# A Mamba-style scan layer in chunks of 512 tokens: the front of a chunk is issued beside the scans of the chunk ahead of it, with its weights streamed from DRAM

## The reference, cut to what matters

```
xn   = layernorm(modulated x)
z    = xn @ W_in                         # 512 channels
gate = silu(xn @ W_gate)
dt   = clip(softplus(z @ W_dt + b_dt), 0.001, 1.0)
Bp, Cp = z @ W_B, z @ W_C                # 16 states each
for t:  h = exp(dt_t * A) * h + dt_t * B_t * z_t      # 512 channels x 16 states
        y_t = sum over states of h * C_t
x1 = x + g * ((y * gate) @ W_out)
```

## Time and profile before

| | us |
|---|---|
| median of 3 runs | 3269.24 (3268.8 to 3269.72) |
| the profiled execution's own time | 3268.99 |
| its span, first to last instruction | 3267.0 |

### The profile page before, as it was taken

How to read it: one execution, slowest core, us unless ns; L and a number is a source line. 1 busy time by engine, 2 the same in 40 slices (tenths; PEclk the granted TensorE clock), 3 DMA queues, 4 the chain that set the end, 5 groups by cost and what they waited for, 6 DMA issues and landing times.

```text
span 3267.0 us, 45469 instructions
## 1 busy us (share of the span) xinstructions
PE 2928.0 (90%) x14848; PEld 2392.1 (73%) x14848; DVE 2684.9 (82%) x4436; ACT 2109.7 (65%) x3852; POOL 1969.2 (60%) x1701
## 2 busy tenths in 40 slices
PE   7576799998999999899999999899999989999898
PEld 4355577787877778687777778777777878777776
DVE  3968989797988979798898979799897979989441
ACT  3555486776758676675767667675866767585443
POOL 1857667475766757565776756566675756666110
PEclk8577699999999999999999999999999999999998
DMA  4241132231422232232313233131332323133122
GB/s 130 82 163 58 50 109 69 98 114 65 141 78 97 76 111 97 87 122 69 110 62 117 91 112 107 65 112 67 111 101 98 107 73 123 59 104 118 46 89 90
DMA packets 152787, 308.56 MB, mean 94 GB/s; under 512 B 18372, under 2 KB 96988, under 8 KB 135144
## 3 DMA queue, kind: packets, MB, share of 16 engines
q1 hardware_dynamic: 152008, 302.52, 27.7%
q0 software_dynamic: 272, 1.57, 0.1%
q10 hardware_dynamic: 272, 1.57, 0.1%
HBM read 288.27 MB, written 17.35 MB: 94 GB/s over the span
## 4 chain that ended last, share of the span: by engine, by line
PE 31%; DVE 28%; issue 18%; ACT 14%; POOL 4%; DMA 2%; DVEq 1%; POOLq 0%; SPq 0%; ACTq 0%
DVE acc L1495 12%; DVE hs L1531 10%; PE ps_B L1771 8%; PE ps_A L1771 7%; PE ps_H L1766 4%; PE ps_H L1784 4%; PE ps_B L1766 3%; ACT ps_A L1302 2%; POOL bu L1151 2%; PE ps_B L1924 2%; PE ps_B L1784 2%; PE ps_B L1876 2%; DVE hA L1725 2%; DMA ws_in<-w_split 1%; ACT nn L727 1%
## 5 line engine op out<-in xcount | busy, mean ns | idle before, releaser
L1151 POOL TENSOR_TENSOR bu<-z,bb 128x512 f32<-128x512 f32 x1024 | 1294.5, 1285 | 344.5 <-DVE hs L1531 286.5
L1531 DVE TENSOR_TENSOR_SCAN hs<-ps_A,state,bu 128x512 f32<-128x512 f32 x768 | 976.1, 1276 | 26.4 <-ACT ps_A L1302 12.9
L1302 ACT ACTIVATE ps_A<-dt,a_neg 128x512 f32<-128x512 f32 x1024 | 700.1, 687 | 450.4 <-DVE hs L1531 448.5
L1766 PE MATMUL ps_H<-ident,hs 128*128 128x128 f32 x4096 | 653.4, 295 | 203.3 <-DVE acc L1495 113.5
L1766 PEld LDWEIGHTS ps_H<-ident,hs 128*128 128x128 f32 x4096 | 522.6, 152 | 348.6 <-DVE acc L1495 151.5
L1495 DVE SCALAR_TENSOR_TENSOR acc<-ps_H,ctok,acc 128x512 f32<-128x512 f32 x960 | 699.5, 730 | 32.7 <-PE ps_H L1766 31.9
L1876 PE MATMUL ps_B<-ws_out,hid 128*128 128x256 f32 x2944 | 694.8, 381 | 2.4 <-ACT hid L1354 2.2
L1876 PEld LDWEIGHTS ps_B<-ws_out,hid 128*128 128x128 f32 x2944 | 535.7, 191 | 66.6 <-ACT hid L1354 2.6
L1771 PE MATMUL ps_B<-fh,ws_in 128*128 128x512 f32 x1440 | 534.8, 417 | 9.2 <-DMA ws_in<-w_split 4.6
L1771 PEld LDWEIGHTS ps_B<-fh,ws_in 128*128 128x128 f32 x1440 | 270.7, 188 | 68.1 <-DVE bl L1686 7.9
L1531 DVE TENSOR_TENSOR_SCAN hs<-ps_A,bu 128x512 f32<-128x512 f32 x256 | 310.5, 1215 | 10.5 <-POOL bu L1151 6.0
(11 more groups left out here) (351 smaller groups left out, 4806.8 us busy)
## 6 DMA issues: line engine op xcount, KB each, us to landing
ws_in<-w_split SPq DMA_DIRECT2D x126, 1024.0 KB, 6.3
bb<-b_rows SPq DMA_DIRECT2D x256, 256.0 KB, 3.6
ws_out<-in_L_ffn_V_rwkv SPq DMA_DIRECT2D x64, 512.0 KB, 5.3
ws_out<-in_L_ffn_W SPq DMA_DIRECT2D x32, 512.0 KB, 8.1
xb<-in_L_attn_x SPq DMA_DIRECT2D x16, 512.0 KB, 6.3
n<-in_L_attn_x SPq DMA_DIRECT2D x16, 512.0 KB, 4.1
w_split<-wsp SPq DMA_DIRECT2D x8, 1024.0 KB, 5.6
out<-xb SPq DMA_DIRECT2D x16, 512.0 KB, 3.0
```

The costliest lines, as they stand in the source:

```text
L1151: pool.tensor_tensor(bu[:, u % 4, :], z[:, d, :], bb[:, s % 2, :], ALU.mult)\
L1302: act.activation(b.t[:, :], dt[:, d, :], ACT.Exp, scale=a_neg[:, d, s:s + 1])\
L1531: dve.tensor_tensor_scan(hs[:, s % 2, d, :], b.t[:, :], bu[:, k % 4, :], state[:, s, d:d + 1] if i % CPB else 0.0, ALU.mult, ALU.add)\
L1766: return pe.transpose(dst, src, ident[:, :])
```

## The change

**Steps.** The marks are gone. A chunk's own list now begins at unit 8. Units 0 to 7 of chunk i+1 are issued among the last steps of chunk i: units 0 to 3 in four new steps "end", each with the last read-out of a channel tile of chunk i, units 4 to 7 in the four y steps. The transposes of state 0 and ACT's copy of them into acc come as four steps "turn0" after out. A chunk has 71 steps instead of 98.

**Front.** Its pieces are due some 20 steps earlier, beside the last units of the chunk ahead (PE: dt and z at -19 to -17 of a step list in which unit 60 is at -19; gates at -10 to -2, after y). The gate products come last.

**Memory.** z, dt and ctok are doubled; bu gets its own buffer; yT is written over gate. The DRAM row buffer of B is doubled. The resident w_in and w_dt are gone: three more slots of 1 MB (dt, z, gt) are written to DRAM once, and read back for every chunk from 1 on, into ws_in[0], ws_in[1], ws_in[0], through SP's queue.

**Banks.** The front's products use B0 and B1, between the experts' up-products and f. 

**Small.** Table loads of ACT are written out for ln, silu, gelu and back to exp/tanh; the bids' Sigmoid becomes Exp(-x) on ACT and an add and a reciprocal on DVE. Chunk 0's norms move from the first block into the second. All PACE values are new.

```diff
-UNIT_STEPS = [("unit", u) for u in range(DS * DB + DB)]
-TAIL_STEPS = [("y", k) for k in range(DB)] + [("out", 0), ("out", 1), ("x1", 0)]
+UNIT_STEPS = [("unit", u) for u in range(2 * DB, DS * DB)]
+END_STEPS = [("end", d) for d in range(DB)]
+TAIL_STEPS = [("y", k) for k in range(DB)] + [("out", 0), ("out", 1), ("x1", 0)] + [("turn0", t) for t in range(NT)]
...
+AT0 = len(UNIT_STEPS) - N_S
...
 BANK_USES = {
-    "A0": FRONT[0::2] + [f"dA{u}" for u in range(0, DS * DB, 2)],
-    "A1": FRONT[1::2] + [f"dA{u}" for u in range(1, DS * DB, 2)],
+    "A0": [f"dA{u}" for u in range(0, DS * DB, 2)],
+    "A1": [f"dA{u}" for u in range(1, DS * DB, 2)],
+    "N0": FRONT[0::2],
+    "N1": FRONT[1::2],
...
-        w_in = {h: sb(f"w_in_{h}", [P, KC, 2 * DI], F32R) for h in "hl"}
-        w_dt = {h: sb(f"w_dt_{h}", [P, KC, DI], F32R) for h in "hl"}
...
-        bu = over("bu", [P, 4, CT], "xnh")
+        bu = sb("bu", [P, 4, CT])
...
-        z = sb("z", [P, DB, CT])
-        dt = sb("dt", [P, DB, CT])
+        z = sb("z", [P, 2 * DB, CT])
+        dt = sb("dt", [P, 2 * DB, CT])
...
-        yT = over("yT", [P, DB, CT], "hs", skip=4 * DB * CT)
+        yT = gate
...
@@ SP, n_stream
+                    for h, name in enumerate(("dt", "z")):
+                        yield name
...
+                            take(sp, i - 3, ("p3", "p7")[h])
+                        front_in(i, name)
+                    yield "bc"
+                    since(sp, s_bu, i - 1)
+                    used(sp, i, "bc")
+                    sp.dma_start(b_rows[i % 2], bcs[DS:2 * DS, :]).then_inc(s_bw.sem, 16)
...
+                    yield "gt"
+                    if i:
+                        take(sp, i, "dt2")
+                        take(sp, i, "dt3")
+                        front_in(i, "gt")
...
@@ ACT, n_stream
+                    for k in range(DB):
+                        yield f"gate{k}"
+                        if k == 0:
+                            load_table(act, "silu")
+                        if i:
+                            take(act, i - 1, "wo0")
+                            take(act, i - 1, "wo1")
...
@@ DVE, step
+                    if name == "end":
+                        if i + 1 < NCH:
+                            scan(i + 1, k)
+                        if i >= 0:
+                            read_out(i, DS - 1, k)
                     if name == "y":
...
+                        if i + 1 < NCH:
+                            scan(i + 1, DB + k)
```

More of the change, by code:

```diff
@@ L48 @@
 NSLOT = len(SLOTS)
+TABLES = {"exp tanh": 0, "exp ln": 6, "gelu": 10, "silu": 18}
+FRONT_SLOTS = ["dt", "z", "gt"]
 CREDIT = 1
@@ new lines, in scan @@
+                def scan(i, k):
+                    s, d = k // DB, k % DB
+                    if d == 0 and s >= 1:
+                        inputs_made(sp, i, s)
+                        if s < DS - 1:
+                            load_b(i, s + 1)
+                        elif i + 1 < NCH:
+                            load_b(i + 1, 0)
+                    if (s, d) == (DS // 4, 1) and i % CPB == 0:
+                        since_x1(sp, i)
+                        sp.dma_start(w_out[:, :, :], kp(w["L0_attn_W_out"])).then_inc(s_wout.sem, 16)
@@ new lines, in step, with front_in @@
+                    if name == "end" and k == 0 and 0 <= i < NCH - 1:
+                        inputs_made(sp, i, DS)
+                        load_b(i + 1, 1)
+                    if name == "y" and i + 1 < NCH:
+                        scan(i + 1, DB + k)
+                def front_in(i, name):
+                    dst = ws_in[1 if name == "z" else 0]
+                    sp.dma_start(dst[:, :, :, :].bitcast(F32).rearrange("p h k m -> p (h k m)"),
+                                 w_split[NSLOT + FRONT_SLOTS.index(name)]).then_inc(s_wf[name].sem, 16)
@@ L1108, in w_stream @@
                 def w_stream(_):
+                    yield "front"
+                    for n, src in enumerate((ws_in[0], ws_in[1], w_gt0)):
+                        sp.dma_start(w_split[NSLOT + n], src[:, :, :, :].bitcast(F32)
+                                     .rearrange("p h k m -> p (h k m)")).then_inc(v_front, 16)
                     yield "fold"
@@ new lines, in keep_state, with scan @@
+                def keep_state(i, s):
+                    for u in (s * DB + DB - 2, s * DB + DB - 1):
+                        used(act, i, f"dA{u}")
+                    act.activation(state[:, s, :], hs[:, s % 2, :, CT - 1], ACT.Copy).then_inc(s_state.sem, 1)
+                def scan(i, k):
+                    s, d = k // DB, k % DB
+                    if d == 2 and s >= 1:
+                        keep_state(i, s - 1)
+                    if s == 0:
+                        act.wait_ge(s_dt.sem, s_dt.at(i, d + 1))
+                    b = fill(act, i, f"dA{k}")
+                    act.activation(b.t[:, :], dt[:, i % 2 * DB + d, :], ACT.Exp, scale=a_neg[:, d, s:s + 1])\
+                       .then_inc(b.full, 1)
@@ L1304, in step @@
[L1304 to L1315 removed]
+                        scan(i, k)
@@ new lines, in step @@
+                    if name == "end":
+                        if k == 2 and i >= 0:
+                            keep_state(i, DS - 1)
+                        if i + 1 < NCH:
+                            scan(i + 1, k)
+                    if name == "y" and i + 1 < NCH:
+                        scan(i + 1, DB + k)
+                    if name == "turn0" and i + 1 < NCH:
+                        b = take(act, i + 1, f"hT{k}")
+                        if k == 0:
+                            used(act, i + 1, "ct")
+                            if i >= 0:
+                                take(act, i, "y2")
+                                take(act, i, "y3")
+                        act.activation(acc[:, k, :], b.t[:, :], ACT.Copy, scale=ctok[:, (i + 1) % 2, k, 0:1])\
+                           .then_inc(b.free, 1)
@@ new lines, in step @@
+                    if name == "end":
+                        if i + 1 < NCH:
+                            scan(i + 1, k)
+                        if i >= 0:
+                            read_out(i, DS - 1, k)
+                    if name == "y":
+                        if i + 1 < NCH:
+                            scan(i + 1, DB + k)
+                        if i >= 0:
+                            used(dve, i, f"gt{k}")
+                            b = take(dve, i, f"y{k}")
+                            dve.tensor_tensor(yT[:, k, :], b.t[:, :], gate[:, k, :], ALU.mult).then_inc(b.free, 1)
```

526 lines of the change are left out of this document (259 added, 267 removed), and 128 rows, old and new, of the table PACE.

## The result

The changed kernel takes 3366.39 us (median of 4 runs, 3358.77 to 3368.56) against 3269.02 for the kernel before on the same chip (3267.75 to 3269.72): a ratio of 1.0294, 95% interval 1.0276 to 1.0312. The forecast was 3124 us with a range of 3060 to 3215. It is slower by 97 us where 145 less were expected. The profiled execution has a span of 3366.0.

A forecast was written before the change was run, and what follows sets the result against it. PE was taken to bound the turn and DVE the scans; overlapping them gives 129.5 + 142 + 13 x 181 + 162 = 2786.5 against 2936.7, saving 150.2, less 5.7 in the head: 3124 us, range 3060 to 3215.

The forecast's parts named there:

- The bound changes hands: Middle chunk: PE ends last at the turn while DVE idles 19 us, DVE in the scans while PE idles 9.3.
- the lower bound is 175.3: Middle chunk: PE's load 175.3 us is the floor, 188.6 the upper bound; PE at 97% gives 181.
- DVE's scans fill its hole at the turn: Turn: eight scans of the next chunk, 10.2 us of DVE work, move into DVE's idle time there.
- PE's front fills its hole at the experts' end: Scans: 13 front products, 17.9 us plus 1.0 of transposes, move from the turn into PE's idle time.
- 129.5 from the first scan: Chunk 0, first scan to gate product: 119.3 us plus eight scans of chunk 1; chunk 1's front hidden by scans.
- Chunk 1, 142: Gate product 0 to 1: DVE bounds it, load stays, DVE fills some 96%; 174.4 us becomes 142.
- ACT at the turn: Rival: unit 8 waits for two ACT table changes, 5.4 us in each of 14 chunks, giving 3200; chance 0.10.
- The last interval, 162: Chunk 15's interval, without front or next scans: PE 156.4 us, at 97% 161, taken as 162.
- Tail unchanged at 241.4: After the last gate product: the same x and f work in the same order, so 241.4 us stays.
- Streaming at zero: Front weights, 3 MB more a chunk, load under cover at no cost; without cover 18.9 us a chunk.
- exposed loads at 3408: Rival: PE stands until weight loads land; all three exposed cost 284 us, giving 3408; chance 0.07.
- Displacement: Rival: front matmuls in the scans delay transposes DVE needs; chunk stays at 188, giving 3215; chance 0.13.

The follow-up runs named there:

- the useless products: Changed kernel plus five groups of eight useless PE products a chunk, ahead of the keys' group and the four transposes behind it; 3319.05 us, ratio 1.0159.
- the run without it: Changed kernel with the second modulation product issued ahead of chunk 0's four gate products, on banks B2 and B3; 3350.39 us, ratio 1.0252.

## Why the prediction was wrong

Point by point, by its own steps:

- **"The bound changes hands ... a chunk costs the sum of both bounds"**, and with it "the lower bound is 175.3 ... I take PE at 97%": this is the step that failed. Busy shares of 93 and 98% were read as two rates that could be evened out. But PE's share at the turn was high because the front stood there, as the one work that waited for almost nobody; take it away and what is left are transposes and short groups, each waiting for the last. PE is busy for 92% of a middle chunk instead of 97, idle for 15.6 us of the turn's 64. Half of the front's products could be dropped, and of the 8.3 us came 1.1 and 2.4. Size: 13 x 10.2 = 133 us of the 242 by which the forecast missed; the head has 26 of them, chunk 1 28, the last interval 19 and the tail 37.
- **"DVE's scans fill its hole at the turn"** came true and was worth nothing: DVE's busy time rose from 47.9 to 51.9 of the turn's 64 us, and a chunk with 3.7 us more of DVE takes no longer.
- **"PE's front fills its hole at the experts' end"** came true in part: the waits for acc fell from 73.8 to 45.6 us over thirteen chunks, and new ones at the turn outweighed them.
- **The granted clock** stood in its own rows (0.80 where DVE closed the experts) and entered no term. The changed kernel could have gained 3.5 us a chunk by it. It is not why the change was slower, for in the middle chunks both kernels have the same mean clock, 0.96 and 0.97. The Trainium skill ("TensorE: Matmul & The Clock Gate", Part 1, The HAM clock gate) says that the throttled state is the default and that activity releases it, and its table "Why this matters for your kernels" advises against gaps of idle time in mid-kernel. By that rule more work at a sparse turn should raise the clock, and the traces agree: 0.82 in the changed kernel, 1.00 with the useless products.
- **Chunk 0, "129.5 from the first scan"**: measured 159.4 (90.7 to 250.1). The first scan came earlier than the 94.6 forecast, at 90.7. The scans then stopped for the modulation product, priced as 5.3 us that "come back": it went in behind the gates on shared banks, stopped DVE for 10.4 and brought its work on the rows with it; its order was worth 16 us in all. Behind it stood the wait for ACT, 13.2 us in the run without it. And five scans, not eight, stand ahead of gate product 0.
- **Chunk 1, 142**: measured 170.0, with DVE busy 137.1 and PE 122.8. The hole at the turn stayed. Here the rival "ACT at the turn" shows bare, with no x stream to hide it, behind two waits for the products out:

```profile
262.81 0.69 DVE L1604 TENSOR_TENSOR xb<-ps_H,xb 128x512 f32<-128x512 f32 x1 [5.74 <-PE ps_H L1848]
266.27 0.69 DVE L1604 TENSOR_TENSOR xb<-ps_H,xb 128x512 f32<-128x512 f32 x1 [2.76 <-PE ps_H L1848]
276.56 1.28 DVE L1578 TENSOR_TENSOR_SCAN hs<-ps_A,state,bu 128x512 f32<-128x512 f32 x1 [7.67 <-ACT ps_A L1336]
```

  The scan of unit 8 waits 7.67 us for ACT, which waits for wo1, the gates and the tables first. In middle chunks DVE's norms of x lie over this, and this scan waits 0.97 us. Over thirteen middle intervals DVE's waits for decay factors came to 68.4 us, none longer than 1.8, as against 10.8 before; no run shows what they cost.
- **The last interval, 162**: 181.3. PE's work was sized nearly right, 161.4 us for 156.4, but it filled 89% instead of 97: the turn's 64 us hold 48.3 of PE, as in a middle chunk.
- **"Tail unchanged at 241.4 ... comes in the same order"**: 278.5, the order was not the same. The diff holds the new due times; they were not read against the old ones. With the old order it is 242.2: the work was priced right.
- **Streaming at zero, POOL's z at zero** were right: without the loads a middle chunk is the same, and with the rows earlier too; over thirteen chunks DVE waits 0.8 us for bu. The rival that was to end on the other side, exposed loads at 3408, came near the number by another road. "Displacement" (a chunk stays at 188) was the nearest in kind, at 3215, and still missed head and tail.
- Its list of signs served: the middle chunk exceeds 186 and the tail moved by more than 15.

## What to carry to other kernels

Before work is moved out of a stretch in which an engine is nearly full, look at what it stands between: if its neighbours there are waits on other engines, it is cover, and its busy time is no bound that falls when it leaves. Price a move from both ends, with the room of the place it goes to (here 3.6 us of it for 7.3 us more of work), and read every written order anew, head and tail too. A cheap test for "has this engine room here?" is to add useless work: some 5 us of it cost 4.6 and 3.5 us a chunk where PE had none, and less than nothing where it had. It doesn't say what taking work away would bring; for that, halve the work in place (2.4 us of 8.3 here).

## What the hardware showed that was not expected

- Useless products made the kernel faster: 40 more instructions a chunk, 6.7 us by their own rows, and 3.5 us a chunk less. The granted clock over the 24 us ahead of the gate product went from 0.82 to 1.00.
- The clock was lost without a long hole: the idle times on PE ahead of 1566.14, where it is at half, are at most 1.95 us each. Between them stand the keys' group and, behind it, transposes alone; whether the holes or the transposes lose it was not separated.
- A program whose chunks are alike can run them at different lengths: 188.5 and 193.5 us, clock 0.96 and 0.93, with all other engines' busy time equal. The interval of one chunk is no measure of an edit; the mean over thirteen is.
